# Masked attention of a four-layer kernel: every mask written by 64x64 tiles of TensorE, a new order of its tasks, and new lags

## What is computed

```python
v = jnp.einsum('nlhd,ed->nlhe', v, Wv)          # 16 heads of 16
k = jnp.einsum('nlhd,ed->nlhe', k, Wk)
q = jnp.einsum('nlhd,ed->nlhe', q, Wq)
energy = jnp.einsum('nqhd,nkhd->nhqk', q, k)
energy = jnp.where(mask == 0, jnp.float32(-1e+20), energy)   # mask: 1 x 1 x 128 x 128
attn = jax.nn.softmax(energy / jnp.sqrt(jnp.float32(embed)), axis=3)
out = jnp.einsum('nhql,nlhd->nqhd', attn, v).reshape(n, q_len, embed)
out = out @ Wo.T + bo
```

## Time and profile before

| | before |
|---|---|
| three runs | 3880.34, 3880.64, 3881.94 us; median 3880.64 us |
| span of the profiled execution | 3869.9 us |
| granted TensorE clock, mean | 0.981 |
| busy: PE, PEld, DVE, ACT, POOL | 3678.2, 2870.0, 3088.5, 2207.4, 2200.5 us |
| masked attention, about | 2380 to 3200 us of the span |

### The profile page before, as it was taken

How to read it: one execution, slowest core, us unless ns; L and a number is a source line. 1 busy time by engine, 2 the same in 40 slices (tenths; PEclk the granted TensorE clock), 3 DMA queues, 4 the chain that set the end, 5 groups by cost and what they waited for, 6 DMA issues and landing times. The chain is left out here.

```text
span 3869.9 us, 134428 instructions
## 1 busy us (share of the span) xinstructions
PE 3678.2 (95%) x47408; PEld 2870.0 (74%) x47408; DVE 3088.5 (80%) x5266; ACT 2207.4 (57%) x4529; POOL 2200.5 (57%) x3316
## 2 busy tenths in 40 slices
PE   5999999995799999999999996999999999999999
PEld 4777777773688888888888884566666668888888
DVE  4888888885778777778777775798888977777777
ACT  3777777775444444444444442577677765555554
POOL 5666666664245443333333334466666667887777
PEclk9999999997899999999999998899999999999999
DMA  4677777774332322222222224799999952232322
GB/s 130 197 204 207 214 209 209 205 213 154 102 85 79 84 68 74 66 70 69 68 72 68 72 66 90 158 211 216 211 217 208 215 151 80 75 77 75 79 75 72
DMA packets 834241, 502.59 MB, mean 130 GB/s; under 512 B 262037, under 2 KB 824408, under 8 KB 833480
## 3 DMA queue, kind: packets, MB, share of 16 engines
q1 hardware_dynamic: 832680, 493.49, 50.5%
q0 software_dynamic: 928, 0.49, 0.1%
HBM read 251.27 MB, written 214.96 MB: 120 GB/s over the span
## 5 line engine op out<-in xcount | busy, mean ns | idle before, releaser
L1556 ACT ACTIVATE phase_spare<-phase_loop_hid,phase_b1T 128x128 f32<-128x128 f32 x2048 | 586.1, 368 | 710.9 <-PE phase_loop_hid L193 702.2
L1129 DVE TENSOR_REDUCE phase_loop_mx<-phase_loop_score 128x8 f32<-128x1024 f32 x512 | 625.4, 1222 | 98.5 <-PE phase_loop_score L882 91.0
L1522 PE MATMUL phase_loop_moe_y<-phase_w,phase_spare 128*128 x2048 | 693.6, 379 | 0.1
L1037 ACT ACTIVATE phase_loop_pt<-phase_loop_scoreT 128x1024 f32<-128x1024 f32 x448 | 458.6, 1024 | 268.3 <-PE phase_loop_scoreT L916 265.8
L1524 PE MATMUL phase_loop_moe_y<-phase_w,phase_spare 128*128 x2048 | 558.2, 273 | 0.0
L191 PE MATMUL phase_loop_hid<-phase_loop_moe_h,all_w_first_hi 128*128 128x128 f16 x2048 | 449.2, 219 | 0.0
L192 PE MATMUL phase_loop_hid<-phase_loop_moe_h,all_w_first_hi 128*128 128x128 f16 x2048 | 449.1, 219 | 0.0
L192 PE MATMUL phase_loop_hid<-phase_loop_moe_h,phase_w_hi 128*128 128x128 f16 x2048 | 449.1, 219 | 0.0
L193 PE MATMUL phase_loop_hid<-phase_loop_moe_h,all_w_first_lo 128*128 128x128 f16 x2048 | 449.1, 219 | 0.0
L193 PE MATMUL phase_loop_hid<-phase_loop_moe_h,phase_w_lo 128*128 128x128 f16 x2048 | 449.1, 219 | 0.0
L191 PE MATMUL phase_loop_hid<-phase_loop_moe_h,phase_w_hi 128*128 128x128 f16 x2048 | 449.0, 219 | 0.0
(11 more groups left out here) (293 smaller groups left out, 11038.9 us busy)
## 6 DMA issues: line engine op xcount, KB each, us to landing
qk_scratch<-phase_loop_qk SPq DMA_DIRECT2D x192, 256.0 KB, 3.4
phase_loop_cin<-in_ctx SPq DMA_DIRECT2D x128, 256.0 KB, 4.6
x_scratch<-phase_loop_x SPq DMA_DIRECT2D x128, 256.0 KB, 3.1
h_scratch<-phase_loop_hr SPq DMA_DIRECT2D x128, 256.0 KB, 3.7
phase_loop_qS<-qk_scratch SPq DMA_DIRECT2D x384, 64.0 KB, 2.8
phase_loop_kS<-qk_scratch SPq DMA_DIRECT2D x384, 64.0 KB, 2.4
ks_scratch<-ct_scratch SPq DMA_DIRECT2D x384, 64.0 KB, 2.4
all_w_first_lo<-ks_scratch SPq DMA_DIRECT2D x128, 192.0 KB, 4.0
```

Source lines behind the costliest of these rows:

```text
L1037: act.activation(pt[n % len(pt)][:, :, :], score_t_bank[:, :].rearrange("p (j n) -> p j n", j=HB2), ACT.Exp, scale=exp_scale).then_inc(s_e ...
L1129: v.tensor_reduce(to, score_bank[:, :].rearrange("p (h j n) -> p h j n", h=2, j=CH), AX.X, ALU.max).then_inc(s_mx.sem, 1)
L1522: pe.matmul(o[:, :], hh[n % NH][:, j, :], row, start=half == 0 and j == 0, stop=False, skip_group_check=True)
L1556: i = act.activation(hf[n % NF][:, j, :], hid(u, n)[:, j * S:(j + 1) * S], ACT.Gelu, bias=w["b1"][:, bass.ds(e * HB + (4 * half + j), 1)], ...
```

## The change

All four groups get their masks on TensorE, in both score layouts, and each mask is now four matmuls of 64 rows by 64 columns in place of two of 128 by 128: two from the mask's own rows into bank 0, and two from a copy with its halves exchanged (`mask_x`, `maskT_x`) crosswise into bank 1. The copies are made by four DMAs of GpSimd in the preparation of layer 2. `cut`, `expo_under`, `keep`, `keep_min` and their steps on DVE, ACT and POOL go. The four mask and score tasks of an n stand together, the `av` tasks stand in pairs, and the f32 transposes are issued in between the matmuls of a projection (`braid`, which takes one matmul of the main task and then as many of the side tasks as `places` says). Every engine's list has a new order and new lags, and `t_y` has `ring0` for itself. In the calls for layer 1 the order is as it was. The core of the diff:

```diff
+def passes(eng, out, l_hi, l_lo, r_hi, r_lo, start, stop, done=None):
+    yield eng.matmul(out, l_hi, r_hi, start=start, stop=False)
+    yield eng.matmul(out, l_hi, r_lo, start=False, stop=False)
+    m = eng.matmul(out, l_lo, r_hi, start=False, stop=stop)
+    if done:
+        m.then_inc(done.sem, 1)
+    yield m
+def braid(count, main, places, *sides):
+    def go(s):
+        def part(lag, task):
+            return task(Unit(0, s - lag)) if 0 <= s - lag < count else iter(())
+        between = chain.from_iterable(part(*side) for side in sides)
+        for i, _ in enumerate(part(*main)):
+            for _ in range(places.count(i)):
+                next(between, None)
+        for _ in between:
+            pass
+    return None, go
...
-            plan = [(8, "t_y"), (4, "t_max"), (1, "q"), (7, "y1"), (6, "y0"), (8, "o")]
-            shared = ((), ("t_max", "q", "o"), ("t_y", "y1", "y0"))
+            plan = [(4, "t_max"), (7, "o"), (6, "y1"), (1, "q"), (5, "y0"), (6, "t_y")]
+            shared = (("t_y",), ("t_max", "o", "q"), ("y1", "y0"))
...
 SP
-                    tasks = [(5, load_c), (1, load_xT), (5, store_max), (3, stack_q), (11, store_x1), (12, store_h),
-                             (2, store_q), (8, load_r), (5, place_max), (2, stack_k)]
+                    tasks = [(2, store_q), (3, load_c), (2, stack_k), (4, store_max), (0, load_xT), (2, stack_q),
+                             (6, load_r), (4, place_max), (7, store_x1), (9, store_h)]
 POOL
-                    tasks = [(11, rows1), (4, maxima), (5, ctx_as_v), (6, cut(p, 3)), (9, rstd1)]
+                    tasks = [(9, rows1), (8, rstd1), (4, ctx_as_v), (3, maxima)]
 PE
+                def mask_tiles(bank, rows, crossed):
+                    for b, part in enumerate((rows, crossed)):
+                        for i in range(2):
+                            k_at, out_at = slice(64 * i, 64 * i + 64), slice(64 * (i ^ b), 64 * (i ^ b) + 64)
+                            pe.matmul(bank[out_at, b * 512:(b + 1) * 512], c["identb"][k_at, k_at], part[k_at, :],
+                                      start=True, stop=False, skip_group_check=True)
...
-                    tasks = [(6, av(0)), (3, score(0)), (8, make["t_y"]), (5, mask_score_t(0)), (4, make["t_max"]),
-                             (5, score_t(0)), (3, mask_score(1)), (6, av(1)), (3, score(1)), (5, score_t(1)),
-                             (1, make["q"]), (7, make["y1"]), (3, mask_score(2)), (5, mask_score_t(2)), (3, score(2)),
-                             (6, av(2)), (5, score_t(2)), (6, av(3)), (3, mask_score(3)), (6, make["y0"]),
-                             (3, score(3)), (5, score_t(3)), (8, make["o"]), (2, mask_score(0))]
+                    tasks = [(3, mask_score(0)), (5, mask_score_t(0)), (3, score(0)), (5, score_t(0)), (6, av(2)), (6, av(3)),
+                             (4, whole(make["t_max"])),
+                             (3, mask_score(1)), (5, mask_score_t(1)), (3, score(1)), (5, score_t(1)),
+                             braid(units, (7, make["o"]), (2, 3, 4, 5), (6, make["y1"])),
+                             (3, mask_score(2)), (5, mask_score_t(2)), (3, score(2)), (5, score_t(2)),
+                             (5, av(0)), (5, av(1)),
+                             (3, mask_score(3)), (5, mask_score_t(3)), (3, score(3)), (5, score_t(3)),
+                             braid(units, (1, make["q"]), (0, 1, 2, 3, 4, 4, 5, 5), (5, make["y0"]), (6, make["t_y"]))]
 ACT
-                    tasks = [(5, copy_max), (6, expo(0)), (6, expo(1)), (2, hi_q), (7, copy_y(0)), (6, expo(2)),
-                             (7, copy_y(1)), (10, norm1), (6, expo(3)), (6, expo_under(3)), (8, hi_y)]
+                    tasks = [(5, expo(0)), (4, copy_max), (6, copy_y(1)), (5, expo(1)), (5, expo(2)),
+                             (8, norm1), (5, copy_y(0)), (5, expo(3)), (1, hi_q), (6, hi_y)]
 DVE
-                    tasks = [(8, norm_y(0)), (10, add_x), (4, row_max(0)), (10, norm1_stats), (9, lo_y),
-                             (4, row_max(1)), (8, norm_y(1)), (2, lo_q), (4, row_max(2)), (6, cut(v, 1)),
-                             (4, row_max(3))]
+                    tasks = [(2, lo_q), (3, row_max(0)), (7, lo_y), (8, norm1_stats), (3, row_max(1)), (6, norm_y(1)),
+                             (7, add_x), (3, row_max(2)), (3, row_max(3)), (5, norm_y(0))]
...
 preparation of layer 2
+        def cross(to, given):
+            g.dma_start(to[0:64, :], given[64:128, :]).then_inc(s_cross, 16)
+            g.dma_start(to[64:128, :], given[0:64, :]).then_inc(s_cross, 16)
+        g.wait_ge(s_v, 1 + CH)
+        cross(w["mask_x"], w["mask"])
+        g.wait_ge(s_turned, CH)
+        cross(w["maskT_x"], w["maskT"])
+        g.wait_ge(s_cross, 64)
...
-        v.tensor_scalar(w["keep"][:, :], b4[:, 0:S // 2].bitcast(BF16), 0.0, None, ALU.is_equal)
-        v.tensor_scalar(w["keep_min"][:, :], b4[:, 0:S // 2].bitcast(BF16), 0.0, KEPT, ALU.is_equal, ALU.mult)
```

More of the change, by code:

```diff
@@ L21 @@
 from contextlib import ExitStack
+from itertools import chain
 import numpy as np
@@ L127, in step @@
         for lag, task in tasks:
-            if 0 <= s - lag < count:
+            if lag is None:
+                task(s)
+            elif 0 <= s - lag < count:
                 task(Unit(0, s - lag))
```

115 lines of the change are left out of this document (48 added, 67 removed).

## The result

The changed kernel takes 3904.94 us (median of four runs, 3900.56 to 3911.61), the kernel before 3880.49 us beside it (3873.28 to 3881.94). The ratio is 1.0068, 95% interval 1.0051 to 1.0084: slower by 0.7%, 24 us. The profiled spans are 3904.1 and 3869.9 us, 34.2 us apart. The changed kernel's profiled execution took 3905.86 us, so only 1.8 us lie around its span. If it was the same before, the profiled execution of before took some 3872 us (an estimate from these 1.8 us), 9 us less than the median of its kernel: most of the 10.7 us that I added was a difference between executions, and it is also why the spans lie further apart than the medians.

What follows compares the result with a forecast made beforehand. TensorE bounds the kernel before, the maxima's round trip the changed one: 60 x (11.5 - 11.6) = -6 us, edges -6, span 3858 us, plus 10.7 us around it: 3868 us, range 3830 to 3912.

Steps and rivals of the forecast that it cites:

- the 10.7 us that I added: Outside the profiled span: the median stands 10.7 us over it, taken as unchanged and added to 3858 us.
- the round trip of the maxima: From PE's `t_max` through SP's store and placing to `score_t(0)`: trip 10.0 us plus 1.47, period 11.5 us.
- the round trip grows: Rival: `load_xT` traffic before the stacking DMAs makes landings of 3.1 us the rule; period 12.1 us, 3905 us; chance 0.19.
- TensorE's own work: PE's step: 11.36 us less 0.74 (masks), 0.15 (order), 0.2 (weaving) is 10.3; with one wait, 10.7 us.
- the wait at `y0`: PE before the woven transposes of `y0`: waits some 0.4 us for ACT's `copy_y(0)`.
- The masks are four abreast: On TensorE: four 64x64 mask matmuls run together, a pair of mask tasks takes 0.54 us, 0.74 us less a unit.
- the rival of two rounds: On TensorE: tiles sharing a bank take turns, masks add 1.76 us, 3908 us; chance of masks not abreast 0.11.
- The placing: SP's issue of `place_max`, which returns the maxima: 5.98 to 7.08 us after `t_max`, 6.7 taken.
- The stacked q: SP's `stack_q`, needed by `score(0)`: q has landed when its turn comes; the next to be late, no time added.
- my signs of being wrong: Placing issued sooner than 6 us or landing under 2.7 (faster); PE waiting at `score(0)` for q, mask pairs 0.9 us (slower).
- Edges: Filling, emptying and layer 2's preparation: shorter lags save 6 us of 0 to 12 in emptying, the rest nothing.
- the slower case: The whole kernel slower than before by more than runs can tell (7.8 us): chance 0.30.

Runs made afterwards that it cites:

- masks_late: The kernel before with all masks as 64x64 tiles, cutting left out, old order and lags, `mask_score_t` right in front of its `score_t`: 3894.0 us, 1.0043 to before.
- q_unwoven: The changed kernel with the maxima's store right behind q's store, and the `y0` and `t_y` transposes behind q's matmuls, not woven in: 3869.4 us, 0.9978 to before.
- max_first: The changed kernel with SP's store of the maxima right behind q's store, and the residual load and `load_xT` behind the placing: 3866.8 us, 0.9971 to before.
- x1_between: The changed kernel with `store_x1` (lag 8) issued between the read of the residual and the placing of the maxima: 3924.0 us, 1.0118 to before.
- less_traffic: The changed kernel with half of the context and residual loads left out, as many transfers issued, outputs not the reference's: 3868.4 us, 0.9977 to before.
- xt_behind: The changed kernel with only SP's `load_xT` moved, behind the placing of the maxima instead of in front of q's stacking: 3870.9 us, 0.999 to before.
- full_masks: The changed kernel with each mask made as before, by two 128 by 128 matmuls instead of four of 64 by 64: 3902.5 us, 1.0073 to before.

## Why the prediction was wrong

The time came out on the other side: 3905 us instead of 3868. The mechanism was right, a period set by the round trip of the maxima, and one term of its sum was too small. The time lies in the range, and it is the number of the rival "the round trip grows"; that is in part luck. The rival's period of 12.1 us is near 12.19, but the kernel spent 5.7 us more in the 60 periods and 4.6 more at the edges than it said, and the 10.7 us around the span, which it took over, were 0.8. Nor did landings grow, as it had it: from the second DMA of the placing they take 3.1 us and more in 25 of 59 units, and did in 24 of 59 before.

*TensorE's own work: the total right, its parts not.* 10.63 us undisturbed, where 10.7 was forecast, and 0.25 us of it is the wait at `y0` that was forecast as 0.4. I gave the masks 0.74 us, the order 0.15 and the weaving 0.2. All masks as tiles in the old order cost 0.42 us (`masks_late`), order with weaving gives 1.15, and the weaving itself gives nothing (`q_unwoven`).

*The masks are four abreast: right,* and the rival of two rounds is out. The Trainium skill (TensorEngine Tiling (Array Packing), Restrictions and Gotchas) has it that different row tiles cannot access one PSUM bank simultaneously. Here tiles of both row halves write to one bank, in different partitions, 0.01 us apart, and the next four start 0.24 us later; the trace does not bear the rule out for this case.

*The placing: the step that failed.* "The placing is issued 5.98 to 7.08 us after `t_max`; I take 6.7." It was 7.25 on the mean, and that is 0.55 of the 0.69 us by which the period was missed. Of these, 0.35 us are the store of the maxima: 0.80 us after `t_max` in one row, but 1.15 on the mean, since in one unit of four SP comes to it late, held up by what stands in front (`store_q`, which waits for DVE, the context, the keys). The other 0.20 us are the stretch from store to placing, 6.10 on the mean where 5.9 was taken, mostly `load_xT` (1.44 us on the mean, 1.25 taken). The late stores were no work of the change: their mean was 1.09 us in before. That trace had the answer. Its placing is issued 7.54 us after `t_max` on the mean, and the prediction's own differences, 1.54 us out and 1.30 in, make 7.30 of it. I built the sum from the row of one unit, and a trip that is the bound is paid at its mean. The other terms held: landing 3.39 us after the first issue (0.6 + 2.73 taken; it is 0.39 + 3.00), 1.46 us from `score_t(0)` to `t_max` (1.47 taken; 1.34 in a usual step, 2618.67 to 2620.01). 7.25 + 3.39 + 1.46 and the 0.05 us to the start make 12.15 us, measured 12.19.

*The stacked q: not priced.* I let it pass with "when its turn comes, q has landed", and that is so in after: the stacking is issued 1.7 us behind the landing. But its own landing is late too, PE waits 23.1 us for it in 400, and it is what binds as soon as the maxima are sooner (`max_first`). A wait of PE at `score(0)` was among my signs of being wrong. In after it costs nothing by itself; it is one reason why no new order of SP's list gained its full price.

*Edges: 6 us in all against 6 later at the start and 7.5 less at the end,* so -1.4 us net.

*The weighting.* One landing in four was late already before, and the forecast left the trip 0.3 us from loss. The rows had a spread of issue times of 1 us: in after, most steps lie anywhere between 11 and 14 us, while before 43 of 60 were 11.36 or 11.37, since TensorE's own work covered the spread. That made the slower case likelier than 0.30.

*What sets the 12.2 us:* shown is the trip of the maxima: its measured terms add up to the period in six runs, which alone is an account and no proof, but `x1_between`, which made only the placing 0.47 us later, made the period 0.39 us longer. The trip of q stands right behind it and binds in `max_first`. The bytes come in through the landings (`less_traffic`). Not settled is what makes a single landing or issue long; and no run moved issues to another engine's queue, so how much SP's one queue costs is open.

## What to carry to other kernels

When an engine is relieved, the period goes to the next round trip, and one that was late in one unit of four has no room. Take the length of such a trip as the mean over all units of the trace, not from one row, because a trip that binds is paid at its mean. Price every arrival that a step begins with (here q, maxima and keys) from the event that starts it, with what stands in front of it in its queue as well as behind, and take queue entries that wait for another engine as gates for all that follow. Before two waits in a row on one engine are called two causes, see which of the two arrivals was later for its need. And see how much the transfers leave: this stage moved 213 GB/s before, and none of the orders tried here got beyond 214 in the same window or below a period of 11.6 us, though TensorE's step was 10.63. Whether another way of issuing would, is not shown.

## What the runs showed of the hardware

- Four 64x64 tiles run abreast, also when two of different row halves write to one PSUM bank in different partitions: the four start within 0.01 us, and the next four 0.24 us later.
- A DMA issue on SP has no fixed length. The same load took 0.51 us and 1.62 us, the two of the keys 0.88 and 1.88 us, one transpose 1.24 to 2.41 us. Fewer bytes shorten the landings (the last stacking 3.6 to 3.0 us with 480 KB a unit less), not these issues.
- The DMA share is no measure of bytes: after has 0.97 at 203 GB/s, `xt_behind` 0.84 at 205 and `max_first` 0.92 at 208, with the same transfers in another order.
- Weaving f32 transposes in among f16 matmuls saved nothing: six matmuls and eight transposes take 1.63 us to the next mask one kind behind the other, and 1.93 woven, 0.25 us of it a wait.
- Busy share of PE says little near a wait: `full_masks` had 192.16 of 200 us, after 178.57, at one period; 1.0 us more work a unit stood where waits had been.
